# First cross layer of two tiles ahead of chunk 0, and a gate applied one step earlier

## What is computed

```python
target = item_id_feat + item_img_feat
seq_emb = item_table[item_seq]                      # 2048 x 50 rows gathered
x = concat([t, seq_emb, t - seq_emb, t * seq_emb])  # t is target, broadcast
scores = (relu(x @ aw1 + ab1) @ aw2 + ab2)          # masked where item_seq == 0
hist_feat = einsum('bs,bsd->bd', softmax(scores), seq_emb)
sparse = stack([like_feat, view_feat, item_id_feat, item_img_feat, hist_feat])
w = sigmoid(relu(mean(sparse) @ se_w1 + se_b1) @ se_w2 + se_b2)   # the gate
se = sparse * w
p = [(se[i] @ bil_W[i]) * se[j] for i < j]          # 10 pairs
dnn_in = concat([se, p])                            # 15 features of 128
xc = dnn_in
for i in range(2):                                  # the two cross layers
    xc = dnn_in * (xc @ cross_K[i] + cross_bias[i]) + xc
h = gelu(ln(xc @ w1 + b1)); h = gelu(ln(h @ w2 + b2))
return sigmoid(h @ w3 + b3)
```

## Time and profile before

| | us |
|---|---|
| median of 3 runs | 2201.66 (2201.39 to 2207.11) |
| the profiled execution | 2186.45 |
| its span | 2184.4 |
| PE busy | 1942.2 (89%) |
| DVE busy | 1330.2 (61%) |
| ACT busy | 899.4 (41%) |
| POOL busy | 904.3 (41%) |
| weight queue (SP) | 136.89 MB of 220.31 MB |

### The profile page before, as it was taken

One profiled execution on the slowest core, in us unless ns is written; L12 is line 12 of the kernel. 1 busy time (PEld: TensorE's weight loads), 2 busy tenths in 40 slices (PEclk: granted clock), 3 DMA queues, 4 the chain that ended last, 5 costly groups with the idle time before them and its releaser, 6 DMA issues. The chain is left out here.

```text
span 2184.4 us, 32774 instructions
## 1 busy us (share of the span) xinstructions
PE 1942.2 (89%) x9609; PEld 1530.2 (70%) x9609; DVE 1330.2 (61%) x2211; ACT 899.4 (41%) x1954; POOL 904.3 (41%) x854
## 2 busy tenths in 40 slices
PE   2654553999999999999999999999999999999995
PEld 1433432777777787777777887777777888888884
DVE  3444444467677766666777766657777654445542
ACT  1333333354444434655444334654445243322222
POOL 6666666566655550455665520555551000000000
PEclk6656655999999999999999999999999999999997
DMA  4111111334343463234343462334333352333330
GB/s 154 45 45 44 42 45 41 101 112 115 111 121 102 134 213 94 80 101 120 103 123 119 123 201 76 98 89 128 118 103 94 115 169 79 92 98 98 99 85 1
DMA packets 99536, 220.31 MB, mean 101 GB/s; under 512 B 21648, under 2 KB 27040, under 8 KB 99232
## 3 DMA queue, kind: packets, MB, share of 16 engines
q1 hardware_dynamic: 62960, 136.89, 21.0%
q0 software_dynamic: 27136, 55.63, 10.1%
q10 hardware_dynamic: 9264, 25.69, 3.1%
HBM read 205.27 MB, written 12.85 MB: 100 GB/s over the span
## 5 line engine op out<-in xcount | busy, mean ns | idle before, releaser
L391 POOL DMA_INDIRECT e<-in_item_table,idx_all x800 | 852.9, 1066 | 689.5 <-issue 334.6
L1056 DVE TENSOR_TENSOR Wl<-raw,Wh 128x640 fp32r<-128x640 f32 (+1 forms) x420 | 338.1, 805 | 293.6 <-DVEq L1055 293.0
L766 ACT ACTIVATE Wh<-raw 128x640 fp32r<-128x640 f32 (+1 forms) x420 | 301.7, 722 | 497.9 <-ACTq L765 494.2
L516 PE MATMUL xps<-X0h,Wh 128*128 128x512 f32 x900 | 365.6, 406 | 6.7 <-PEq L514 6.7
L516 PE MATMUL xps<-X1h,Wh 128*128 128x512 f32 x900 | 359.6, 400 | 0.0
L518 PE MATMUL xps<-X0h,Wl 128*128 128x512 f32 x900 | 353.7, 393 | 0.0
L517 PE MATMUL xps<-X0l,Wh 128*128 128x512 f32 x900 | 352.9, 392 | 0.0
L518 PE MATMUL xps<-X1h,Wl 128*128 128x512 f32 x900 | 351.4, 390 | 0.0
L517 PE MATMUL xps<-X1l,Wh 128*128 128x512 f32 x900 | 351.1, 390 | 0.0
L729 ACT ACTIVATE e<-e,pw 128x128 f32<-128x128 f32 x800 | 242.6, 388 | 15.4 <-ACTq L122 15.4
L433 PE MATMUL aps<-ident,e 128*128 128x128 f32 x700 | 111.9, 295 | 106.8 <-issue 90.4
(11 more groups left out here) (145 smaller groups left out, 2227.0 us busy)
## 6 DMA issues: line engine op xcount, KB each, us to landing
raw<-in_cross_K SPq DMA_DIRECT2D x360, 320.0 KB, 2.9
raw<-in_w SPq DMA_DIRECT2D x60, 256.0 KB, 2.7
e<-in_item_table,idx_all POOLq DMA_INDIRECT x800
dnn_scratch<-dn ACTq DMA_DIRECT2D x12, 960.0 KB, 4.5
x1f<-dnn_scratch ACTq DMA_DIRECT2D x3, 2048.0 KB, 9.7
x1f<-dnn_scratch ACTq DMA_DIRECT2D x3, 1792.0 KB, 15.4
dn<-in_embT SPq DMA_DIRECT2D x1, 1024.0 KB, 5.3
img_scratch<-dn ACTq DMA_DIRECT2D x1, 1024.0 KB, 5.3
```

The costliest lines, as they stand in the source:

```text
L391: nc.gpsimd.indirect_dma_start(out=dst, out_offset=None, in_=table, in_offset=bass.IndirectOffsetOnAxis(ap=idx_all[:, t, s:s + 1], axis=0) ...
L516: m0 = mm(out, wh, Xh[:, 0:T, k, :], start=(k == 0), stop=False)
L766: af(Wh[:, split_slot(w), 0:n], raw[:, rs, 0:n], ACT.Copy).then_inc(hi_done, 1)
L1056: v.tensor_tensor(Wl[:, rs, 0:n], raw[:, rs, 0:n], Wh[:, slot, 0:n].bitcast(F32), ALU.subtract).then_inc(lo_done, 1)
```

## The change

The plan is new. The opening does three tiles only (`OPEN_TILES = 3`), in 17 steps. Then come 15 early steps, marked `early`: layer one of the cross layers for tiles 0 and 1 alone, 256 columns wide, with all 45 weight blocks of that layer fetched and split for it (`EXTRA = 45` units at the head of the weight stream). The first 15 steps of chunk 0 then do layer one of tiles 2 and 3 alone, also 256 wide, with the same 45 blocks once more; its other 15 steps and all later chunks are 512 wide as before. The groups stand so: tile 2's last group in early step 0; tile 3's in early steps 1, 3, 5, 7, 9; tile 4's in early steps 11 and 13 and steps 1, 3, 5 of chunk 0; tile 5's in steps 7, 8, 9, 11, 12; tile 6's in 14 to 18; tile 7's in 20 to 24. For chunks 1 and 2 nothing moves.

For the tiles of chunk 0 the gate is applied in the step of the fold, and lift and pair come one step earlier (`late` is 0); for the others they stay. In the last opening step the transposes and the score use the banks that the cross products don't use. POOL waits after every ten gathers only for tiles below `OPEN_TILES`.

```diff
+EARLY = 2
+EXTRA = FEATS * UNITS
+LEAD = 3
+OPEN_TILES = 3
+OPEN_STEPS = LEAD + NG * OPEN_TILES - 1
+EARLY_AT = OPEN_STEPS
+CHUNK_AT = EARLY_AT + FEATS
+def group_steps():
+    where = [[LEAD + NG * j + g for g in range(NG)] for j in range(OPEN_TILES)]
+    where.append([EARLY_AT + k for k in (1, 3, 5, 7, 9)])
+    where.append([EARLY_AT + k for k in (11, 13)] + [CHUNK_AT + k for k in (1, 3, 5)])
+    where += [[CHUNK_AT + k for k in ks] for ks in ((7, 8, 9, 11, 12), (14, 15, 16, 17, 18), (20, 21, 22, 23, 24))]
+    for c in range(1, CHUNKS - 1):
+        where += [[CHUNK_AT + STEPS * c + 1 + 6 * j + g for g in range(NG)] for j in range(4)]
 def make_plan():
-    lead = 3
-    open_steps = lead + NG * TILES[0] + 5
+    for k in range(FEATS):
+        plan.append(Step(0, k, (0, EARLY), k * UNITS))
+        plan[-1].early = True
     for c in range(CHUNKS):
-        plan += [Step(c, k) for k in range(STEPS)]
+        for k in range(STEPS):
+            tiles = (EARLY if c == 0 and k < FEATS else 0, TILES[c])
+            plan.append(Step(c, k, tiles, EXTRA + c * STREAM + k * UNITS))
...
-        plan[last + 2].fold = plan[last + 3].gate = plan[last + 4].lift = plan[last + 5].pair = t
+        late = 0 if t < TILES[0] else 1
+        plan[last + 2].fold = plan[last + 2 + late].gate = plan[last + 3 + late].lift = plan[last + 4 + late].pair = t
...
-                        if (s + 1) % (GRP if t < TILES[0] else SUB) == 0:
+                        if (s + 1) % (GRP if t < OPEN_TILES else SUB) == 0:
...
-                    m0 = mm(out, wh, Xh[:, 0:T, k, :], start=(k == 0), stop=False)
-                    m1 = mm(out, wh, Xl[:, 0:T, k, :], start=False, stop=False)
-                    m2 = mm(out, wl, Xh[:, 0:T, k, :], start=False, stop=(k == FEATS - 1))
+                    m0 = mm(out, wh, Xh[:, a:b, k, :], start=(k == 0), stop=False)
+                    m1 = mm(out, wh, Xl[:, a:b, k, :], start=False, stop=False)
+                    m2 = mm(out, wl, Xh[:, a:b, k, :], start=False, stop=(k == FEATS - 1))
...
-                if p.grp:
+                if p.last:
+                    transposes(*p.grp, 0)
+                    transposes(*p.grp, 1)
+                    score()
+                elif p.grp:
...
+            for p in early:
+                step(p)
             for c in range(CHUNKS):
...
-                if p.gate is not None:
-                    tail_gate_apply(p.gate)
                 if p.summed:
                     history(*p.summed)
                 if p.fold is not None:
                     tail_fold(p.fold)
+                if p.gate is not None:
+                    tail_gate_apply(p.gate)
```

More of the change, by code:

```diff
@@ L64, with __init__ @@
 STEPS = 2 * FEATS
[L67 to L71, removed]
+EARLY = 2
[12 more added lines that the diff above has]
+        where += [[CHUNK_AT + STEPS * c + 1 + 6 * j + g for g in range(NG)] for j in range(4)]
+    return where
 class Step:
-    def __init__(self, chunk, k):
-        self.chunk, self.k = chunk, k
+    def __init__(self, chunk, k, tiles=None, first=None):
+        self.chunk, self.k, self.tiles, self.first = chunk, k, tiles, first
         self.layer, self.n = (None, None) if chunk is None else divmod(k, FEATS)
+        self.early = self.last = False
+        self.prev = None
         self.grp = self.open = self.summed = None
@@ L601, in opening_step @@
                 if p.open:
-                    hidden(shared=False)
+                    hidden(shared=p.last)
                 if p.pair is not None:
@@ L616, in step @@
                 T, k = p.fc, p.k
-                products(p.chunk, p.layer, p.n, 0)
+                products(p, 0)
                 if T and 2 <= k < T + 2:
@@ L625, in step @@
                     transposes(*p.grp, 0)
-                products(p.chunk, p.layer, p.n, 1)
+                products(p, 1)
                 if p.grp:
@@ L637, in step @@
                     fc_w3(T)
-                products(p.chunk, p.layer, p.n, 2)
+                products(p, 2)
                 if T and 2 <= k < T + 2:
@@ L848, in step @@
                     weigh(p.summed[1])
-                if p.n or p.layer:
-                    x_hi(*((c, p.layer, p.n - 1) if p.n else (c, 0, FEATS - 1)))
-                if p.gate is not None:
+                if p.prev:
+                    x_hi(p.prev)
+                if p.gate is not None and p.fold is None:
                     tail_gate()
@@ L1176, in step @@
                 c, k, T = p.chunk, p.k, p.fc
[L1177 removed]
+                prev = p.prev
                 if c and k == 0:
```

185 lines of the change are left out of this document (101 added, 84 removed).

## The result

The changed kernel took **2222.52 us** (median of 5, 2222.30 to 2228.48) beside 2207.11 for the kernel before on the same chip (median of 5, 2201.39 to 2212.36): ratio 1.0081, 95% interval 1.0061 to 1.0100. By the ratio it is some 18 us slower; the medians are 15.4 apart. The forecast was 2204.5 (+2.8 us) with a range of 2187 to 2222: a change too small to measure was held most likely (0.49), slower next (0.31). The time lies just outside the range. That it is outside at all is in part chance, since the kernel before, whose median the forecast took as 2201.66, was 5.5 us slower in this comparison.

A forecast was written before the change was run, and what follows sets the result against it. POOL's gathers were taken to set the pace to tile 7's last transposes. +11.6 there, -10.2 for one wide step less and +1.4 for the clock gave +2.8 us, added to 2201.66: 2204.5 us, range 2187 to 2222.

The forecast's parts named there:

- tile 7's last transposes, with the clock: End of tile 7's gathering in chunk 0: transposes at 731.0 instead of 719.4, +11.6 us, plus 1.4 for lower clock.
- one wide step less, and the steps up to the last: Chunk 0 behind those transposes: they stand in step 24 instead of 23, so one wide step less follows, -10.2 us.
- chunk 1 to the end: From chunk 1 on: all as before, with the same distances, 0 us.
- Narrow products: Early layer and chunk 0's first 15 steps: 256-wide products every 0.12 us, a step 5.4 us instead of 10.2.
- POOL's pace: Gathers of tiles 3 to 7: 96.2 us each for tiles 3 and 4, 284.6 for 5 to 7, ending at 729.3.
- the third rival: Narrow steps: 256-wide products get no cheaper, 0.227 us each, PE arrives at 770, +40, 2242 us; chance 0.09.
- The quiet pace: Rival, tiles 3 to 7: POOL gathers a tile in 91.5 us, ending at 707.4; -20.6, 2181 us; chance 0.22.
- the slowest: Rival, tiles 3 to 7: POOL takes 99.0 us a tile, ending at 744.9; +18.3, 2220 us; chance 0.19.
- the signs named for "right": Tiles 3 to 7: PE waits before nearly every group's transposes, gathers never wait for `e_free`, last gather near 729.
- PE could be there at 630: PE's sum to tile 7's last transposes, from 251.6: narrow steps 157, wide ones 95, attention 118 us.
- POOL decides: Tile 7's last transposes: POOL's data allow them at 731.0, 101 us after PE could be there.
- Tile 7's store slips, the w1 units hide it: End of chunk 0: the store moves from step 28 to 29, may slip 2 or 3 us, hidden by w1 splits, 0.

The follow-up runs named there:

- second trace: Trace of the unaltered changed kernel on a second chip: 2200.22 us beside 2190.81 for the kernel before, ratio 1.0046.
- third trace: Trace of the unaltered changed kernel on a third chip: 2199.87 us beside 2190.39 for the kernel before, ratio 1.0052.
- tens to tile 7: Changed kernel, POOL waiting after every ten gathers for tiles 3 to 7, tiles 5 to 7 in the kernel before's steps: 2195.76 us, ratio 1.0040.
- first trace: Trace of the unaltered changed kernel on the first chip: 2222.52 us beside 2207.11 for the kernel before, ratio 1.0081.
- regular places: Changed kernel with groups of tiles 5 to 7 in chunk 0's steps 7 to 11, 13 to 17, 19 to 23, as before: 2205.69 us, ratio 1.0092.
- the gate alone: Kernel before with only the gate moved into the fold's step in the opening, lift and pair one step earlier: 2188.03 us, ratio 1.0006.
- one row weighted: Changed kernel with ACT weighting one of a group's ten rows in narrow steps, all orders kept: 2197.01 us, ratio 1.0034.
- Five reorderings: Changed kernel with ACT's or DVE's order altered in narrow steps, the last two also with POOL waits and places altered: ratios 1.0167, 1.0104, 1.0071, 1.0020, 1.0085.

## Why the prediction was wrong

The ledger is made on the chip on which both kernels were traced in one round: spans 2185.1 and 2197.0, 11.9 apart.

```profile
718.90 0.76 PE L433 MATMUL aps<-ident,e 128*128 128x128 f32 x5
...
784.23:835.23 51.00, 51.00 (x227) 42.24 (x225) 30.20 (x46) 20.08 (x34) 17.81 (x16) 1.00 0.64 214
835.23:2185.10 1349.87, 1307.55 (x6464) 1046.17 (x6462) 844.53 (x1372) 579.56 (x1177) 399.92 (x368) 0.99 0.35 104
```

and the changed kernel:

```profile
734.96 0.55 PE L467 MATMUL aps<-ident,e 128*128 128x128 f32 x3
...
789.05:842.79 53.74, 52.31 (x236) 43.14 (x235) 32.52 (x49) 22.11 (x38) 23.89 (x23) 1.00 0.65 212
842.79:2197.00 1354.21, 1309.87 (x6464) 1047.74 (x6462) 844.17 (x1372) 579.49 (x1177) 396.20 (x368) 0.98 0.35 104
```

| term | forecast | this chip |
|---|---|---|
| tile 7's last transposes, with the clock | +11.6 + 1.4 | +16.1 |
| one wide step less, and the steps up to the last | -10.2 | -11.2 |
| chunk 0's last step and the w1 stage | 0 | +2.7 |
| chunk 1 to the end | 0 | +4.3 |
| sum | +2.8 | +11.9 |

Of the 9.1 us between the two sums, 3.1 lie ahead of tile 7's last transposes, 2.7 in the w1 stage and 4.3 behind it; -1.0 is the second term. The first of these looks small only because of a coincidence, told below.

- **Narrow products: right.** They start every 0.12 us, and a narrow step without a group takes 5.48 (5.4 forecast). Not dear, and the third rival is out. By the formula of the Trainium skill (TensorE: Matmul & The Clock Gate, "Back-to-back issue gap") for a product by itself at the higher clock the gap is 109 ns at this width; the rows above show 0.12 us.
- **POOL's pace: right.** Tile 7's last gather ended at 723.8, 730.4 and 732.9 in three traces; forecast 729.3. Tiles 3 to 6 took 93.5 to 96.7 us each in the second trace (forecast 96.2). The quiet pace (707 at tile 7) did not come, nor the slowest (745). Of the signs named for "right", POOL's gathers never waited for `e_free` in the second and third trace; in the first they did, for 17.3 us in all. PE's waits for gathers before nearly every group did not come.
- **"PE could be there at 630": this step failed.** With POOL out of its way (tens to tile 7) PE is there at 720.3 and 723.5. I had put a narrow step at its products and a tile's attention at 24.5, the price among wide steps, and so took it that the attention would hide its handovers (one engine's wait for the other's result) behind products as it did there. The narrow step holds half the products: 1.8 us between the two halves of a group against 3.4 us and more of ACT's work in one queue, and against DVE's fold and gate where a tile closes. Taking 2.7 us of that work out of ACT's queue, with POOL out of the way, brought PE there at 700.8: that the weighting is one part is shown, DVE's part is read from the trace and was not taken off by itself. In the third trace the 340.5 us of narrow steps hold 66 us of waiting, and PE's busy time is stretched by a clock of 0.90. I had read PE's full row before as a property of the attention; it was one of the wide steps.
- **"POOL decides": wrong, by a few us.** PE's chain ended at 733.7 to 735.0 (749.2 in the first trace), POOL's data at 732 to 734.5. Two sums of quite different making came out within 3 us of each other. That is why the forecast of this term was off by 3 only although its reason was wrong, and why each experiment that took off one of them showed little.
- **The places.** Putting tile 7's last group in step 24 instead of 23 costs the 2.7 us in the w1 stage that I had called hidden: in the kernels with regular places that stretch is 51.0 again. "Tile 7's store slips, the w1 units hide it" is a term mis-sized at zero.
- **From chunk 1 on: zero was wrong.** Each of the changed kernel's traces, and of its variants, shows 1351.7 to 1354.8 (1362.4 in the first), before 1348.7 and 1349.9, and the gate alone 1348.1. In chunk 2's step 20 both kernels wait before a group, before for 1.8 us and the changed one for 1.9, with the same instructions; the first keeps the clock, the second loses it behind the wait:

```profile
1610.60:1627.47 16.87, 15.04 (x83) 11.32 (x81) 12.27 (x21) 4.13 (x7) 10.43 (x9) 1.00 0.34 95
...
1621.00:1639.51 18.51, 16.61 (x83) 12.48 (x81) 13.53 (x25) 4.24 (x7) 11.06 (x12) 0.91 0.34 92
```

The first row is before, the second the changed kernel: 1.6 us. The third trace has four such stretches from chunk 1 up to the last steps, the second trace of before two; that accounts for some 3.3 of the 4.3 us on this chip. In the changed kernel's second trace there are three (1354.5 us), in the first of before one (1348.7), so the count explains a part only. The rest, and why the clock falls more often, stays open.

**The rivals.** The slower rival that I named (POOL at its slowest, 2220) gives nearly the time measured first by the wrong mechanism. The right one, that narrow steps do not cover the handovers of the attention, was not among them, though the trace of before had the pieces: ACT's weighting of 3 us and 15 products' time.

**What stays open.** On the first chip the difference was 18 us, on two others 10 and 11.5. The first trace shows the narrow steps 17 to 19 us longer with the same instructions. One place of it, in step 17, on ACT:

```profile
459.25 1.37 ACT L807 ACTIVATE Wh<-raw 128x640 fp32r<-128x640 f32 x2 [3.65 <-ACTq L806]
```

L807 copies weight blocks, here two. The first copy waits for the first product of the step's last unit, which PE began at 455.91 by the trace; in the second trace the same copy began 0.4 us behind its product, here 3.3. The block itself was not late: the last packet of it ended 5.6 us before the copy. DVE's softmax, the weighting and PE's wait (4.65 instead of 2.30) are late by the same 3 us. There are eight such delays of over 1.4 us in the narrow steps of the first trace and one in those of the second; what makes them, and whether it is the chip, was not settled.

## What to carry to other kernels

- A stage's price per unit of side work (here 24.5 us a tile) holds only for the main work it is woven into. When the main step is halved, sum the in-order queue of each helper engine between two handovers again: one step of PE's products must be longer than it.
- Before "X decides", work out the other chain with its handovers, not with busy times. Where two limits end within some us of each other, taking off one can show nothing; an experiment that takes off both tells.
- Five reorderings of ACT's and DVE's queues moved the wait to the next engine in the ring, and none made the narrow steps more than 6 us shorter. Less work in the ring (here 2.7 us of ACT) made them 17 to 23 us shorter.

## What the runs showed of the hardware

- Of two waits of 2.3 us in successive pairs of the second trace (steps 18 and 20) one was followed by 3.4 us at the 1.2 GHz level (products every 0.21 instead of 0.12 us), the other was not; with one row weighted, where waits in those pairs were 1.1 us at most, the clock stayed at 1.00. In chunk 2 it was 1.8 against 1.9 us. Length does not decide it: in chunk 1 the kernel before waited 1.15 us in its first trace and kept the clock, and 1.16 us before the same instructions in its second, where 3.4 us at the 1.2 GHz level followed. So a short wait of PE costs its own length and at times 1.6 us more, and the same code can fall on either side.
- Waiting for gathers after every ten instead of every five took tile 7's last gather from 730 to 694 (tiles 3 to 7 of the changed kernel, regular places). Tiles 3, 4, 6 and 7 took 82.5 to 86.0 us each, against 93.5 to 98.8 with waits after every five (second trace); tile 5 took 105.7, as POOL then waited for the buffer that the attention had not freed.
